# Two histograms by one-hot matmuls: one-hot matrices laid out in pairs of columns

## The reference, cut to what matters

```
deg  = segment_sum(ones_like(dst), dst, num_segments=n)      # graph convolution, with self loops
dinv = rsqrt(max(deg, 1));  norm = dinv[src] * dinv[dst]
out  = segment_sum((h @ w_gcn.T)[src] * norm[:, None], dst, num_segments=n) + b_gcn
...
e     = leaky_relu(a_src[src] + a_dst[dst])                  # graph attention
alpha = exp(e - segment_max(e, dst)[dst]) / segment_sum(...)[dst]
agg   = segment_sum(h[src] * alpha, dst) + b_gat
```

## Time and profile before

| | |
|---|---|
| runs | 6403.15 us median of three (6402.35 to 6422.75) |
| profiled execution | 6419.1 us, its span 6417.1 us |
| mean granted TensorE clock in it | 0.748 of full speed |
| PE | 4381.1 us busy (68% of the span), 14757 matmuls |
| VectorE | 2724.0 us (42%) |
| ScalarE | 759.1 us (12%) |
| POOL | 2976.3 us (46%) |
| DMA | 531.23 MB, 83 GB/s on average |

### The profile page before, as it was taken

One profiled execution on the slowest core, in us unless ns is written; L12 is line 12 of the kernel. 1 busy time (PEld: TensorE's weight loads), 2 busy tenths in 40 slices (PEclk: granted clock), 3 DMA queues, 4 the chain that ended last, 5 costly groups with the idle time before them and its releaser, 6 DMA issues. The chain is left out here.

```text
span 6417.1 us, 45813 instructions
## 1 busy us (share of the span) xinstructions
PE 4381.1 (68%) x14757; PEld 2842.7 (44%) x14757; DVE 2724.0 (42%) x5225; ACT 759.1 (12%) x1439; POOL 2976.3 (46%) x2919
## 2 busy tenths in 40 slices
PE   6998777788688887787755324954954774773067
PEld 4776544444455555555545112632622442441045
DVE  6786566565555456666555000211211211221255
ACT  1113311222100000000001000110210110110022
POOL 0000467667656557777720774146146326334500
PEclk8667988889878877777765556966966886885588
DMA  2112433333345543333465211211211211221168
GB/s 70 52 52 56 142 111 116 112 111 118 107 128 150 138 126 97 89 89 90 87 123 154 53 9 25 68 25 35 68 25 35 52 41 35 51 44 28 23 158 218
DMA packets 241828, 531.23 MB, mean 83 GB/s; under 512 B 73332, under 2 KB 147415, under 8 KB 234822
## 3 DMA queue, kind: packets, MB, share of 16 engines
q1 hardware_dynamic: 121909, 293.42, 16.8%
q0 software_dynamic: 119696, 235.05, 15.7%
HBM read 377.97 MB, written 150.28 MB: 82 GB/s over the span
## 5 line engine op out<-in xcount | busy, mean ns | idle before, releaser
L933 POOL DMA_INDIRECT g_rows<-table,gcn_srcT x1664 | 1780.5, 1070 | 778.3 <-issue 477.9
L1794 POOL DMA_INDIRECT n_rows<-gtab,so_own x1122 | 1082.8, 965 | 1255.0 <-DVEq L1911 913.8
L1742 PE MATMUL p_py<-f_w,f_hh 128*125 128x256 f32 x2688 | 723.1, 407 | 778.6 <-issue 778.6
L1003 PE MATMUL g_ps<-g_rows,g_hot 128*125 128x256 f32 x3328 | 1085.9, 465 | 224.9 <-issue 151.9
L1288 DVE TENSOR_TENSOR acc<-acc,g_ps 125x256 f32 x1664 | 697.5, 419 | 908.8 <-PE g_ps L1003 463.7
L1742 PEld LDWEIGHTS p_py<-f_w,f_hh 128*125 128x125 f32 x2688 | 539.3, 201 | 984.0 <-issue 921.6
L1935 DVE TENSOR_TENSOR p_ob<-p_py,p_xb 125x512 f32<-125x512 f32 x168 | 114.6, 691 | 1982.2 <-remote 924.4
L1003 PEld LDWEIGHTS g_ps<-g_rows,g_hot 128*125 128x125 f32 x3328 | 711.5, 229 | 505.9 <-issue 340.9
L1736 PE MATMUL p_ph<-f_xfT,f_w 128*128 128x500 f32 x1344 | 656.2, 630 | 279.6 <-issue 211.1
L1736 PEld LDWEIGHTS p_ph<-f_xfT,f_w 128*128 128x128 f32 x1344 | 271.5, 202 | 625.5 <-issue 620.3
L1964 ACT ACTIVATE f_hh<-p_ph,f_b 128x500 f32<-128x500 f32 x336 | 224.8, 677 | 1965.8 <-remote 1142.2
(11 more groups left out here) (329 smaller groups left out, 4119.9 us busy)
## 6 DMA issues: line engine op xcount, KB each, us to landing
o_d<-p_ob SPq DMA_DIRECT2D x21, 1920.0 KB
z_ob<-o_d SPq DMA_DIRECT2D x21, 1920.0 KB
g_rows<-table,gcn_srcT POOLq DMA_INDIRECT x1664
n_rows<-gtab,so_own POOLq DMA_INDIRECT x1122
gout<-n_o SPq DMA_DIRECT2D x11, 1224.0 KB
xnT_d<-a_xnT SPq DMA_DIRECT2D x25, 500.0 KB, 2.9
m_area<-xnT_d SPq DMA_DIRECT2D x25, 500.0 KB
qT_d<-m_area SPq DMA_DIRECT2D x25, 500.0 KB
```

The source lines that it names most:

```text
L933: pool.indirect_dma_start(out=rows[:, g % RING, j], out_offset=None, in_=K.table, in_offset=bass.IndirectOffsetOnAxis(ap=K.gcn_srcT[:, 4 * ...
L1003: mm = pe.matmul(ps[q, p % 4, b], hot[:, g % 4, 2 * j + b], rows[:, g % RING, 2 * j + b], start=True, stop=True, skip_group_check=True)
L1742: mm = pe.matmul(py[0:TN, e % 2, j // 2, (j % 2) * D:(j % 2 + 1) * D], self.hh[:, e % 2, c, j * TN:(j + 1) * TN], self.w2[:, e, c], start= ...
L1794: pool.indirect_dma_start(out=rows[:, c % 3, j], out_offset=None, in_=K.gtab, in_offset=bass.IndirectOffsetOnAxis(ap=K.gat_src[:, c * W + ...
```

## The change

Both one-hot matrices of both histograms get one layout: (pair, number or tile, two columns). The 16 columns of a round form 8 pairs; within a pair the two columns' elements lie side by side for each number (or tile). A matmul that takes one column reads its elements in steps of 4 bytes, in `on` (before: 32 bytes) and in `ot` (before: 2 bytes). VectorE writes in runs of two, and both comparisons now have the same form: the table `number`, now each number written twice (250 elements), read once for each of the 8 pairs, against the two ids of the pair, read again for each number. `ot` no longer reads `iota_h`, but the first 200 elements of `number`. The number of elements in each build, the instructions on every engine, their order, their semaphores and all DMAs are as before; the one instruction with another size is the copy that makes `number` (250 elements in place of 2000), in both histograms.

```
-        on = K.so_x[:, 0, 0:TN * HB].bitcast(BF16).rearrange("p (s n b) -> p s n b", s=2, b=HB)
-        ot = K.so_x[:, 1, 0:NT * HB].bitcast(BF16).rearrange("p (s b n) -> p s b n", s=2, b=HB)
-        number = K.so_own[:, 0:TN * HB // 2].bitcast(BF16).rearrange("p (n b) -> p n b", b=HB)
+        on, ot = (K.so_x[:, a, 0:n * HB].bitcast(BF16).rearrange("p (s g n b) -> p s g n b", s=2, g=HB // 2, b=2)
+                  for a, n in ((0, TN), (1, NT)))
+        number = K.so_own[:, 0:TN].bitcast(BF16).rearrange("p (n b) -> p n b", b=2)
...
                     for b in range(HB):
-                        mm = pe.matmul(pdeg[0:NT, 0, q], ot[0:c, r % 2, b], on[0:c, r % 2, :, b], start=r == 0 and b == 0,
+                        mm = pe.matmul(pdeg[0:NT, 0, q], ot[0:c, r % 2, b // 2, :, b % 2],
+                                       on[0:c, r % 2, b // 2, :, b % 2], start=r == 0 and b == 0,
                                        stop=r == rounds - 1 and b == HB - 1)
...
-                    dve.tensor_tensor(on[0:c, r % 2], number[0:c], K.gcn_node[0:c, cols].unsqueeze(1).to_broadcast([c, TN, HB]),
-                                      ALU.is_equal).then_inc(node_s, 1)
-
-                    wide = [c, HB, NT]
-                    dve.tensor_tensor(ot[0:c, r % 2], K.iota_h[0:c, 0:NT].unsqueeze(1).to_broadcast(wide),
-                                      K.gcn_tile[0:c, cols].unsqueeze(2).to_broadcast(wide), ALU.is_equal).then_inc(tile_s, 1)
+                    for out, ids, width, sem in ((on, K.gcn_node, TN, node_s), (ot, K.gcn_tile, NT, tile_s)):
+                        wide = [c, HB // 2, width, 2]
+                        dve.tensor_tensor(out[0:c, r % 2], number[0:c, 0:width].unsqueeze(1).to_broadcast(wide),
+                                          ids[0:c, cols].rearrange("p (g b) -> p g b", b=2).unsqueeze(2).to_broadcast(wide),
+                                          ALU.is_equal).then_inc(sem, 1)
...
-                dve.tensor_copy(number, K.iota_h[:, 0:TN].unsqueeze(2).to_broadcast([P, TN, HB])).then_inc(numbered, 1)
+                dve.tensor_copy(number, K.iota_h[:, 0:TN].unsqueeze(2).to_broadcast([P, TN, 2])).then_inc(numbered, 1)
```

More of the change, by code:

```diff
@@ L869, in gather_mix @@
         node_h = part(2560, 512).bitcast(BF16)
-        number = part(3072, 1000).bitcast(BF16).rearrange("p (n b) -> p n b", b=HB)
-        on = part(4072, 2000).bitcast(BF16).rearrange("p (s n b) -> p s n b", s=2, b=HB)
-        ot = part(6072, 1600).bitcast(BF16).rearrange("p (s b n) -> p s b n", s=2, b=HB)
+        number = part(3072, TN).bitcast(BF16).rearrange("p (n b) -> p n b", b=2)
+        on = part(4072, 2000).bitcast(BF16).rearrange("p (s g n b) -> p s g n b", s=2, g=HB // 2, b=2)
+        ot = part(6072, 1600).bitcast(BF16).rearrange("p (s g n b) -> p s g n b", s=2, g=HB // 2, b=2)
         by_tile = part(7672, TN)
@@ L1092, in degrees @@
                     for b in range(b0, b0 + 4):
-                        mm = pe.matmul(pa[0:NT, q], ot[:, r % 2, b], on[:, r % 2, :, b], start=r == 0 and b == 0,
+                        mm = pe.matmul(pa[0:NT, q], ot[:, r % 2, b // 2, :, b % 2],
+                                       on[:, r % 2, b // 2, :, b % 2], start=r == 0 and b == 0,
                                        stop=r == half - 1 and b == HB - 1)
@@ L1355, in degrees @@
                         dve.wait_ge(used, r - 1)
[L1356 to L1362, removed]
+                    out, ids, width, sem = ((on, node_h, TN, node_s), (ot, tile_h, NT, tile_s))[at]
+                    wide = [P, HB // 2, width, 2]
+                    dve.tensor_tensor(out[:, r % 2], number[:, 0:width].unsqueeze(1).to_broadcast(wide),
+                                      ids[:, cols].rearrange("p (g b) -> p g b", b=2).unsqueeze(2).to_broadcast(wide),
+                                      ALU.is_equal).then_inc(sem, 1)
                 def numbers(i):
@@ L1372, in numbers @@
                     if i == 2:
-                        dve.tensor_copy(number[:], K.iota_h[:, q].unsqueeze(2).to_broadcast([P, TN, HB])).then_inc(id_s, 1)
+                        dve.tensor_copy(number[:], K.iota_h[:, q].unsqueeze(2).to_broadcast([P, TN, 2])).then_inc(id_s, 1)
                         dve.wait_ge(id_s, 4)
```

## The result

The changed kernel took 6224.48 us (median of four runs, 6206.17 to 6237.9), beside 6412.95 us for the kernel before in the same session (four runs, 6402.35 to 6455.88). The ratio is 0.970, with a 95% interval of 0.967 to 0.973: 3.0% faster. The profiled execution took 6223.8 us (span 6221.8), 195 us less than the profiled one of before. Forecast were 221 us.

What follows compares the result with a forecast made beforehand. PE was taken to bound the first histogram and POOL's row gathers the second. Savings of 177 (first histogram), 40 (second) and 4 us (copies) made 221, so 6403 - 221 = 6182 us, range 6130 to 6335.

Steps and rivals of the forecast that it cites:

- PE's part: First histogram: one-hot matmuls in 4-byte steps start every 0.107 us at half clock; PE's block 12.8 us.
- The float32 rows: Profile rows of float32 matmuls, elements 4 bytes apart, about 0.10 or 0.21 us each; nearest rows for PE's new pace.
- rival 3: 4-byte steps cost PE two clocks a column; first histogram's block 19.4 us at half clock: 6332 us; chance 0.07.
- rival 4: PE isn't faster at all; first histogram's block stays 20.48 us: 6359 us; chance 0.04.
- VectorE's part: First histogram: "ot" build falls from 1818 to 990 ns, "on" stays 1199; VectorE's block 12.94 us.
- rival 2: VectorE's pairs work, but the hop after each pair costs, 1.74 ns a tick: 6359 us; chance 0.06.
- rival 5: Run of two loses VectorE's "on" build its double pace, 2240 ns: slower, 6451 us; chance 0.05.
- rival 1: VectorE keeps one element a tick for "ot"; its block stays 16.26 us: 6294 us; chance 0.06.
- The sum for the first histogram: PE and VectorE nearly tie; 25 blocks fall from 20.48 to 13.4 us, saving 177 us.
- The sum for the second histogram: Shorter "ot" builds hold POOL's gathers less, saving 40 us; bounds 0 and 53.
- The copies: Table of numbers shrinks in both histograms; copies of 2.24 and 2.23 us become about 0.4, together 3.6 us.
- theory D: Follow-up theory for POOL's waits in the second histogram: something lets a gather through only every 1.45 us, whatever else runs.

Runs made afterwards that it cites:

- second half alone: Kernel before with only the second histogram changed to the new layout, the first left old: 6424.48 us, ratio 0.998.
- "on" as before: Changed kernel, but in the second histogram only "ot" in pairs and "on" in its old layout: 6231.46 us, ratio 0.970 to the kernel before.
- changed again: The changed kernel run again, nothing altered, beside the others on one chip: 6212.35 us, ratio 0.966 to the kernel before.
- first half alone: Kernel before with only the first histogram changed: 6237.97 us, ratio 0.972; on another chip 5072.08 us, ratio 0.962.
- first four experiments: First histogram changed alone, second alone, both but the second's "on" old, and the changed kernel again: 6237.97, 6424.48, 6231.46, 6212.35 us.

## Why the prediction was right, and where it was not

The forecast of 6182 us missed the median of 6224.48 by 42; the kernel before was itself 10 us slower in that session, so the gain was 188 to 195 us where 221 stood. The direction, the order of the terms and the range (6130 to 6335) held. That the total came so near owes something to luck: the first histogram gave 17 us more than its term, the second 14 to 29 less. The forecast's own range of 6145 to 6225 doesn't follow from the bounds given for it: a block of 12.9 and 53 us from POOL make 6156, a block of 14.4 and none make 6247.

- **PE's part: right, and better than said.** Columns in 4-byte steps take 0.059 us from start to start at full clock, with the bound from below at 0.052, and 0.105 at half clock, where 0.107 was forecast. The float32 rows had nothing to do with it; rival 3 (two clocks a column) and rival 4 (no gain) fall. What was taken too low is the clock. I counted with the level of half speed in much of the block; the granted clock of the stretch is 0.90, after 0.66 before, and 1.00 through the block shown (253 to 266 us).
- **VectorE's part: right.** "ot" was put at 990 ns and is 984; "on" was kept at 1199 and is 1191. Its work in a block was put at 12.94 us and is 12.64: the 16.26 us read from the kernel before were 0.3 too many, as the run with the old "ot", which VectorE fills, shows with 15.97. Runs of two neighbours are enough for two elements a tick, and a word that is read again and again costs nothing. Rivals 1, 2 and 5 fall; the run with the old "ot" shows the block that rival 1 would have had, 15.97 us for its 16.26. The rule on adjacent words in the Trainium skill (Vector Engine (DVE) Microarchitecture Reference, 5.2 Measured stream behaviour on trn2), which stood behind rival 2, isn't borne out by these builds as rival 2 applied it: 0.52 ns an element with one repeated word as an operand.
- **The sum for the first histogram: the term was too small.** 177 us were forecast, from a block of 13.4. From the first build to the last one-hot matmul it was 521.8 us and is 327.7: 194 us, 7.76 a block. (The first gather starts 196 us earlier; the copy is the other 2.) The blocks average 12.8 us once they run evenly. The waiting that was to lift 12.94 to 13.4 hardly came, because PE at full clock is mostly far enough ahead: VectorE's waits in the whole histogram are 4.4 us. The run in groups of four, with the slower pace, has just that waiting and 13.65 us.
- **The sum for the second histogram: the step that failed.** POOL is held 54 us less, more than the 40 I took and about the upper bound of 53. But where the kernel before takes the predicted 6400 us, this gave 12 us. The step took it for certain that POOL, once let go, goes on at 1.25 us a gather. The rows behind it showed almost no waits, and I read that as room. There was hardly any: with the holds halved, 15 waits of 3 to 4 us appear, 47 us in all. Four profiles with the new second half on the chips where before takes 6400 us (after, second half alone, "on" as before, changed again) have 47, 51, 50 and 51 us of them; the two with the old second half have 5 and 9. The four stretches take 1.45 to 1.46 us a gather, the two old ones 1.47 and 1.48. By the times of whole kernels on one chip, the second half was worth 11 us (alone) and 26 us (on top of the first half). On the two other chips the waits are absent, and the term, measured on one of them, is worth 45 to 49 us, close to the 40 forecast.
- **The copies: right in length.** 2.24 and 2.23 us became 0.41 each, 3.7 us together. The first is on the path (the first build starts 1.7 us earlier); whether the second is can't be told, since it lies in the gathers that took 11 us longer.

One of the waits looks like this (changed kernel; PE, VectorE and POOL):

```profile
2384.92 1.08 PE L1004 MATMUL g_ps<-g_rows,g_hot 128*125 128x256 f32 x4
...
2395.66 0.26 PE L1094 MATMUL m_pa<-m_area 128*100 128x125 bf16 x1 [0.43 <-issue]
...
2396.36 0.26 PE L1094 MATMUL m_pa<-m_area 128*100 128x125 bf16 x1 [0.44 <-issue]
2397.05 0.94 POOL L934 DMA_INDIRECT g_rows<-table,gcn_srcT  x1 [0.30 <-issue]
2397.76 0.22 PE L1094 MATMUL m_pa<-m_area 128*100 128x125 bf16 x1 [1.14 <-issue]
2400.69 0.98 DVE L1290 TENSOR_TENSOR acc<-acc,g_ps 125x256 f32 x2 [7.27 <-remote]
2400.82 0.95 POOL L934 DMA_INDIRECT g_rows<-table,gcn_srcT  x1 [2.82 <-remote]
```

The add at 2400.69 takes the sum of the matmuls that PE had by 2386.00 in the records, so PE's signal seems to have come some 14 us after its work. POOL's next gather, which waits for the same matmuls to free its buffer, starts 0.13 us after the add. In between PE issues single matmuls 0.7 us apart (one is missing from the records before 2397.76), waiting for nothing that the profile shows.

One could think that POOL's longer holds had covered such delays in the kernel before. The traces don't bear that out, since VectorE's adds show the late signals too, whether POOL waits or not. Their waits in the histogram's stretch, before and after:

```profile
DVE acc L1288 <- remote: 9.2, 3, 5.4
DVE acc L1290 <- remote: 164.7, 29, 12.0
```

In the stretch of the 512 gathers, 11 of some 256 adds of the kernel before begin over 5 us after the last of their matmuls, in two groups, and these are where POOL's two waits are. With the first half alone it is 19 adds in three groups; in the four profiles with the new second half on such chips, 73 to 87 in 16 to 18 groups. On the two other chips no add of this stretch begins more than 2.1 us after its matmul. So most of the late signals came with the new second half and were not there to be covered. They are no new thing in the kernel, though: among the 550 or so adds ahead of the histogram, 65 to 77 are that late in all six profiles, and 2 to 4 on the two other chips.

The waits stand 35 to 52 us apart in the changed kernel, 205 to 304 of PE's recorded instructions, most often 256, and the profile has one transfer of 16 KB of code for each 256 or so; but the kernel before, and the changed kernel on the other chip, have the same 16 transfers in this stretch and two waits or none, so this is no more than a coincidence that would be worth a test. What delays PE's signals there stays open: the runs made to settle it met a chip that doesn't show them. A bound of about 1.45 us a gather (theory D), just under the pace that the kernel before had, fits the six stretches and was not tested. Shown is that the waits were there in all four profiles with the new second half where before takes 6400 us and in none where it takes 5260, and that there the second half is worth a quarter to a little over half of the 45 us that it is worth elsewhere.

## What to carry to other kernels

Where PE wants single columns of a bf16 operand and VectorE wants runs, lay it out in pairs: at full clock steps of 4 bytes are near PE's full pace, 8 bytes cost double, 16 or more four times as much (at half clock 8 bytes cost a tenth more, 16 or more double), and a run of two keeps VectorE's double pace. Price such a step at both levels of the clock, since a PE that is relieved may be granted the higher one. Where an engine is held less, a profile without waits is no proof that it will go faster: another limit may lie just below its pace, as here at 1.45 us a gather under 1.47, so look for a stretch that already runs at the pace you count on.

## What the runs showed of the hardware that was not expected

The same kernel takes 6397 to 6461 us in the session of the result and on the chip of the first four experiments, and 5256 to 5280 on two other chips, with the first histogram as long everywhere (blocks of 20.48 us before and 12.6 to 13.0 after). The difference lies in the gathers and above all in the last part, where PE works through the experts: the 1104 gathers ahead of the histogram take 1723 to 1760 us in the first case and 1511 to 1532 in the second, and after the last gather the rest of the changed kernel takes 3162 us and 2238. Whether the chip itself or something else about these sessions makes the difference isn't shown. The same line of PE in a stretch of 1000 us (3300 to 4300), the changed kernel on a chip of each kind:

```profile
L1742 PE MATMUL p_py<-f_w,f_hh 128*125 128x256 f32 x840 | 248.4, 422 | 371.7 <-issue 371.6
```
```profile
L1742 PE MATMUL p_py<-f_w,f_hh 128*125 128x256 f32 x2222 | 488.1, 379 | 0.0
```

In the one PE stands idle for 0.44 us before each matmul, with nothing to wait for that the profile shows; in the other never. A change that relieves an engine can therefore be worth 45 us on one chip and 11 to 26 on the next, with the same instructions.
